# Keys evicted from PSUM once as f32 and split in SBUF, and one weighted sum per odd slot put in front of the transposed scores

## The reference

```python
x = _layernorm(x + attn(x, w_qkv, w_out, w_c1, w_c2))        # causal, rope, 56 tokens
x = _layernorm(x + xattn(x, ctx_2048, wq, bq, wkv, bkv, wp, bp))
x = _layernorm(x + ffn(x, gate_w, gate_b, w1, b1, w2, b2))   # top 2 of 8 experts

def xattn(x, cond, ...):                       # x (16, 56, 256), cond (16, 1500, 256)
    q = _qdq(x) @ _qdq(wq).T + bq              # int8 grid, as floats
    k, v = jnp.split(cond @ wkv.T + bkv, 2, axis=-1)
    # 16 heads of 16
    attn = jax.nn.softmax(jnp.einsum('bnhd,bmhd->bhnm', q, k) * scale, axis=-1)
    o = jnp.einsum('bhnm,bmhd->bnhd', attn, v)
    return _qdq(o) @ _qdq(wp).T + bp
```

## Time and profile before

| | |
|---|---|
| median of 3 runs | 853.0 us (848.32 to 858.43) |
| profiled execution, its own time | 854.35 us |
| its span, first to last instruction | 852.5 us |
| busy: PE, DVE, ACT, POOL | 774.4, 638.2, 511.5, 296.9 us |
| granted PE clock, mean | 0.986 |
| cross-attention, about | 50 to 690 us |

### The profile page before, as it was taken

The page is one execution under the profiler, slowest core; times in us unless marked ns, Lnnn a source line. Parts: engine busy times, 40 slices in busy tenths (PEclk is TensorE's granted clock), DMA queues, the critical chain, the costliest instruction groups (busy, mean ns, idle before and its releaser), DMA issues.

```text
span 852.5 us, 30042 instructions
## 1 busy us (share of the span) xinstructions
PE 774.4 (91%) x12379; PEld 582.8 (68%) x12379; DVE 638.2 (75%) x1234; ACT 511.5 (60%) x1084; POOL 296.9 (35%) x366
## 2 busy tenths in 40 slices
PE   5689989999998999999999999999898899999996
PEld 3366666576666666666666666666665579999995
DVE  5877777868877878785977778786875745688887
ACT  2347656566565657655665666666665543787772
POOL 3263216223712371254126421732270003143232
PEclk9899999999999999999999999999999899999999
DMA  7356554554645546554655655565467976766643
GB/s 228 91 167 174 169 155 139 156 160 128 179 129 159 164 143 180 164 143 138 178 156 141 173 169 147 154 171 156 121 186 208 307 258 161 225 190 209 210 136 98
DMA packets 91380, 143.27 MB, mean 168 GB/s; under 512 B 11423, under 2 KB 79583, under 8 KB 87918
## 3 DMA queue, kind: packets, MB, share of 16 engines
q1 hardware_dynamic: 87742, 136.74, 53.6%
q0 software_dynamic: 3504, 4.62, 2.8%
HBM read 101.60 MB, written 39.68 MB: 166 GB/s over the span
## 4 chain that ended last, share of the span: by engine, by line
PE 57%; DVE 13%; DMA 11%; ACT 10%; issue 6%; SPq 1%; POOL 1%; DVEq 0%; POOLq 0%; ACTq 0%
PE ps L1659 15%; PE ps L1652 11%; DMA sums<-y_sb,g_token 10%; PE ps L1733 7%; PE ps L1711 6%; DVE negmax L522 4%; ACT pT L1441 3%; ACT k_front L1414 3%; PE ps L1971 3%; PE ps L1675 3%; DVE k_front L516 2%; PE ps L1992 2%; PE ps L1776 2%; PE ps L1620 2%; PE ps L1743 2%
## 5 line engine op out<-in xcount | busy, mean ns | idle before, releaser
L522 DVE TENSOR_REDUCE negmax<-ps 112x1 f32<-112x1500 f32 x121 | 207.4, 1714 | 32.1 <-PE ps L1675 31.9
L1441 ACT ACTIVATE pT<-ps 125x448 f32<-125x448 f32 x384 | 195.7, 546 | 21.9 <-PE ps L1711 18.2
L1265 POOL TENSOR_TENSOR ctx_lo<-ctx_raw,ctx_hi 128x250 f16<-128x250 f32 x188 | 119.3, 666 | 182.4 <-DVE ctx_hi L507 182.4
L1711 PE MATMUL ps<-qbd,k_st 97*128 97x112 f16 x1536 | 127.8, 214 | 17.3 <-ACT pT L1441 8.7
L1711 PEld LDWEIGHTS ps<-qbd,k_st 97*128 97x128 f16 x1536 | 91.2, 98 | 73.6 <-ACT pT L1441 20.1
L1397 ACT COPY v_sb<-ps 125x512 f32<-125x512 f32 x96 | 56.4, 587 | 83.5 <-PE ps L1659 83.4
L516 DVE SCALAR_TENSOR_TENSOR k_front<-ps,bk_sb,k_front 128x500 f16<-128x500 f32 x80 | 58.8, 735 | 63.0 <-ACT k_front L1414 63.0
L1733 PE MATMUL ps<-pT,v_sb 125*17 125x56 f32 x6144 | 92.1, 215 | 12.2 <-issue 12.2
L1733 PEld LDWEIGHTS ps<-pT,v_sb 125*17 125x17 f32 x6144 | 79.9, 98 | 31.9 <-issue 20.1
L1414 ACT ACTIVATE k_front<-ps,bk_sb 128x500 f16<-128x500 f32 x80 | 54.3, 678 | 62.3 <-PE ps L1652 62.3
L1659 PE MATMUL ps<-wkv_hi,ctx_hi 128*125 128x256 f16 x384 | 76.6, 281 | 10.5 <-DVE k_front L516 9.0
(11 more groups left out here) (263 smaller groups left out, 1492.7 us busy)
## 6 DMA issues: line engine op xcount, KB each, us to landing
k_st<-k_dram SPq DMA_DIRECT2D x288, 125.0 KB, 3.0
w_sb<-w SPq DMA_DIRECT2D x25, 1024.0 KB, 5.2
ctx_raw<-ctx_T SPq DMA_DIRECT2D x48, 500.0 KB, 3.7
k_dram<-k_front SPq DMA_DIRECT2D x80, 250.0 KB, 3.0
xs<-zeros SPq DMA_DIRECT2D x28, 260.0 KB, 4.4
w_sb<-w SPq DMA_DIRECT2D x8, 512.0 KB, 5.2
k_dram<-k_back SPq DMA_DIRECT2D x16, 250.0 KB, 2.9
xg<-xs SPq DMA_DIRECT2D x21, 130.0 KB, 4.1
```

The lines of the kernel that those rows point to most:

```text
L522: V.tensor_reduce(negmax[0:QW], ps[0:QW, BANK_S:BANK_S + CHUNKS, 0:MC], AX.XY, ALU.max, negate=True).then_inc(max_done, 1)
L1265: last = nc.gpsimd.tensor_tensor(ctx_lo[:, k, c2, a], ctx_raw[:, k, c2, a], ctx_hi[:, k, c2, a], ALU.subtract)
L1441: nc.scalar.activation(pT[0:MT, (PAIRS * b + p) % 3, TPC * g:TPC * g + TPC], ps[0:MT, BANK_T + n % 2, 0:TPC * QW].rearrange("p (t n) -> p ...
L1711: last = mm(ps[:, BANK_T + n % 2, QW * i:QW * i + QW], k_st[:, j, p, a:a + P], qbd[:, j, p].rearrange("p h s -> p (h s)"), start=True, sto ...
```

## The change

1. ACT evicts a key unit once, as f32 with its bias, into `k_full` (three buffers), and this alone frees the PSUM bank.
2. DVE copies `k_full` to f16 for the high part; the low part is `k_full` minus the high part, both in SBUF. GpSimd makes it in two halves of 250 columns (`k_lo_step`), but DVE does for batch 0 (`key_low`), and for units 0 and 2 of every odd batch: both together in slot 3 of the even batch before, behind the maximum of pair 3.
3. The parts go into three buffers `k_two` instead of six. A store now waits for the low part (`k_lo_done`), the high part for the store of three keys before, ACT for the low part of three keys before.
4. In odd slots PE does the weighted sum of pair p - 2 in front of the transposed scores; only that of pair p - 1 stays behind the unit. Slot 3 of even batches keeps the old order.

```diff
@@ -159,14 +159,15 @@
         a_xqT = sb("a_xqT", [P, CH, P], BF16)
         wkv_hi = sb("wkv_hi", [P, CH, 2 * D], F16)
         wkv_lo = sb("wkv_lo", [P, CH, 2 * D], F16)
-        k_front = sb("k_front", [P, 5, 2, MC], F16)
+        k_two = sb("k_two", [P, 3, 2, MC], F16)
+        k_full01 = sb("k_full01", [P, 2, MC])
         sb("behind_k_front", [P, 8], F32)
         ctx_raw = sb("ctx_raw", [P, 2, CH, MC])
         ctx_hi = sb("ctx_hi", [P, 2, CH, MC], F16)
         ctx_lo = sb("ctx_lo", [P, 2, CH, MC], F16)
         q_st = sb("q_st", [KS, PAIRS, P], F16)
         k_st = sb("k_st", [KA, 2, PAIRS, M + 4], F16)
-        k_back = sb("k_back", [P, 2, MC], F16)
+        k_full2 = sb("k_full2", [P, MC])
         sb("behind_keys", [P, 616])
         q_mx = sb("q_mx", [KS, 2, PAIRS, 2, S], F16)
         v_sb = sb("v_sb", [P, 2, M // MT, H, VW])
...
@@ -219,7 +220,7 @@
         b_x2T = a_t2[:, 0:D].rearrange("p (c n) -> p c n", c=CH)
         b_oqT = a_t2[:, D:D + P].bitcast(BF16).rearrange("p (c n) -> p c n", c=CH)
-        k_two = [k_front[:, n] for n in range(5)] + [k_back]
+        k_full = [k_full01[:, 0], k_full01[:, 1], k_full2]
         staging = pT[:].rearrange("p a m n -> p (a m n)")
         wkv_raw = staging[:, 0:CH * 2 * D].rearrange("p (c n) -> p c n", c=CH)
...
@@ -433,10 +435,13 @@
             return CH * c + g
-        def stored(b, u):
-            n = KEY_UNITS.index(u)
-            return k_out[n % 2], 16 * (len(KEY_UNITS) // 2 * b + n // 2 + 1)
+        def key_number(b, u):
+            return len(KEY_UNITS) * b + KEY_UNITS.index(u)
+        def stored(n):
+            return k_out[n % 2], 16 * (n // 2 + 1)
         def loaded(b):
...
@@ -509,12 +514,21 @@
             def unit_step(b, par, u):
                 c, g = UNIT[u]
                 if g in KEYS:
-                    i = key_place(c, g)
-                    dve.wait_ge(unit_done, UNITS * b + u + 1)
-                    dve.wait_ge(k_hi_done, len(KEY_UNITS) * b + KEY_UNITS.index(u) + 1)
-                    V.scalar_tensor_tensor(k_two[i][:, 1], ps[:, BANK_KV, 0:MC], bk_sb[:, g:g + 1], k_two[i][:, 0],
-                                           ALU.add, ALU.subtract).then_inc(unit_out, 1)
+                    n = key_number(b, u)
+                    dve.wait_ge(unit_out, UNITS * b + u + 1)
+                    if n >= 3:
+                        dve.wait_ge(*stored(n - 3))
+                    V.tensor_copy(k_two[:, n % 3, 0], k_full[n % 3]).then_inc(k_hi_done, 1)
+                    if b == 0:
+                        key_low(b, u)
+            def key_low(b, u):
+                n = key_number(b, u)
+                dve.wait_ge(k_hi_done, n + 1)
+                dve.wait_ge(k_lo_done, n)
+                V.tensor_tensor(k_two[:, n % 3, 1], k_full[n % 3], k_two[:, n % 3, 0], ALU.subtract).then_inc(k_lo_done, 1)
             def max_step(b, p):
                 n = PAIRS * b + p + 1
...
@@ -859,6 +873,10 @@
                     if units_on:
                         for u in unit_slots(slot):
                             unit_step(b + 1, 1 - j, u)
+                    if slot == 3 and j == 0:
+                        key_low(b + 1, 0)
+                        key_low(b + 1, 2)
                     if t_before is not None:
                         b_tail(bt_behind, t_before)
                     if slot == 1 and units_on:
...
@@ -1080,11 +1098,11 @@
             def store_keys(b, u, between=()):
                 c, g = UNIT[u]
-                i = key_place(c, g)
-                sp.wait_ge(unit_out, UNITS * b + u + 1)
+                i, n = key_place(c, g), key_number(b, u)
+                sp.wait_ge(k_lo_done, n + 1)
                 if not (isinstance(b, int) and b == 0):
                     sp.wait_ge(k_in[g], loaded(b - 1))
-                sp.dma_start(k_dram[i], k_two[i]).then_inc(stored(b, u)[0], 16)
+                sp.dma_start(k_dram[i], k_two[:, n % 3]).then_inc(stored(n)[0], 16)
                 for dst, src in between:
                     sp.dma_start(dst, src).then_inc(w2_ahead, 16)
...
@@ -1325,23 +1347,46 @@
             pool.wait_ge(set_pe, 5)
             nc.gpsimd.memset(v_sb[:, 1, :, :, DH:VW], W_UP).then_inc(ones_v, 1)
+            def k_lo_step(b, u):
+                n = key_number(b, u)
+                pool.wait_ge(k_hi_done, n + 1)
+                if b % 2 == 1 and u == 5:
+                    pool.wait_ge(k_lo_done, n)
+                for half in range(2):
+                    a = slice(MC // 2 * half, MC // 2 * half + MC // 2)
+                    last = nc.gpsimd.tensor_tensor(k_two[:, n % 3, 1, a], k_full[n % 3][:, a], k_two[:, n % 3, 0, a], ALU.subtract)
+                last.then_inc(k_lo_done, 1)
             def iteration(it, t_before):
-                ctx_lo_step(2 * it + 1, 1, 1)
+                b = 2 * it + 1
+                ctx_lo_step(b, 1, 1)
                 if it > 1:
                     scatter(it - 2)
                 if it > 0:
                     pool.wait_ge(b_oq_done, it)
                 kbd_step(it + 1)
-                ctx_lo_step(2 * it + 1, 1, 2)
-                ctx_lo_step(2 * it + 2, 0, 0)
+                ctx_lo_step(b, 1, 2)
+                k_lo_step(b, 5)
+                k_lo_step(b, 6)
+                k_lo_step(b, 8)
+                ctx_lo_step(b + 1, 0, 0)
                 if t_before is not None:
                     b_rstd_step(t_before)
-                ctx_lo_step(2 * it + 2, 0, 1)
+                k_lo_step(b, 11)
+                ctx_lo_step(b + 1, 0, 1)
+                k_lo_step(b + 1, 0)
+                k_lo_step(b + 1, 2)
                 rstd_step(it + 1)
-                ctx_lo_step(2 * it + 2, 0, 2)
+                ctx_lo_step(b + 1, 0, 2)
+                k_lo_step(b + 1, 5)
+                k_lo_step(b + 1, 6)
+                k_lo_step(b + 1, 8)
                 qbd_step(it + 1, 0, 0)
-                ctx_lo_step(2 * it + 3, 1, 0)
+                ctx_lo_step(b + 2, 1, 0)
                 qbd_step(it + 1, 0, 1)
+                k_lo_step(b + 1, 11)
                 for h in range(2):
                     qbd_step(it + 1, 1, h)
...
@@ -1373,7 +1418,10 @@
             ctx_lo_step(B - 1, 1, 1)
             scatter(TILES - 3)
             ctx_lo_step(B - 1, 1, 2)
+            k_lo_step(B - 1, 5)
             b_rstd_step(TILES - 2)
+            for u in (6, 8, 11):
+                k_lo_step(B - 1, u)
             scatter(TILES - 2)
             pool.wait_ge(sums_set, 16 * TILES)
...
@@ -1406,13 +1454,12 @@
             def k_hi_step(b, u):
                 c, g = UNIT[u]
-                i = key_place(c, g)
-                if b > 0:
-                    act.wait_ge(*stored(b - 1, u))
+                n = key_number(b, u)
                 act.wait_ge(unit_done, UNITS * b + u + 1)
-                nc.scalar.activation(k_two[i][:, 0], ps[:, BANK_KV, 0:MC], ACT.Identity,
-                                     bias=bk_sb[:, g:g + 1]).then_inc(k_hi_done, 1)
+                if n >= 3:
+                    act.wait_ge(k_lo_done, n - 2)
+                nc.scalar.activation(k_full[n % 3], ps[:, BANK_KV, 0:MC], ACT.Identity, bias=bk_sb[:, g:g + 1]).then_inc(unit_out, 1)
             def v_step(b, par, u):
...
@@ -1897,6 +1944,11 @@
                         if t_before is not None:
                             b_over(2 if PAIRS * j + slot == 8 else B_SLOTS.get(PAIRS * j + slot - 1, -1), t_before)
                         a_step(A_AT.get(PAIRS * j + slot, -1), t_next)
+                    if not even and not (slot == 3 and j == 0):
+                        if p > 0:
+                            pv(b, j, p - 2)
+                        elif b > 0:
+                            pv(b - 1, 1 - j, PAIRS - 2)
                     scores_T(b, j, p, 0)
                     scores_T(b, j, p, 1)
                     if slot == 2 and j == 0 and b > 0:
...
@@ -1909,7 +1961,7 @@
                     else:
                         for u in us:
                             unit(b + 1, 1 - j, u)
-                        for q in (p - 2, p - 1):
+                        for q in (p - 2, p - 1) if slot == 3 and j == 0 else (p - 1,):
                             if q >= 0:
                                 pv(b, j, q)
                             elif b > 0:
```

9 lines of the change are left out of this document (7 added, 2 removed).

## The result

| | before | after |
|---|---|---|
| median, us | 853.3 (848.3 to 858.4, 4 runs) | 892.0 (888.7 to 893.1, 4 runs) |
| ratio | | 1.0447 (95% interval 1.0379 to 1.0515) |
| profiled execution, us | 854.35, span 852.5 | 888.71, span 886.9 |
| granted clock, mean | 0.986 | 0.959 |

The kernel became slower by 38.7 us. The forecast was 878, the range 852 to 897.

The account below looks back on a forecast made before the run. PE's own work plus a few short gaps per batch was taken to bound the kernel. Gains - 28, stops + 38, other waits + 2 and clock + 13 gave + 25 on 854.35: 879, or 878 on the median's scale; range 852 to 897.

Parts of the forecast that it names:

- The stop: Slot 4 of even batches: PE's scores wait for unit 11's load behind unit 0's store; 4.5 us, 7 times, 38 with batch 14.
- I take 1.36: 312.92: Batch 6, slot 3: DVE's low part beside GpSimd's work takes 1.36 us and ends at 312.92 on the trace's clock.
- the 3.7 without contention: Lower bound of the slot 4 stop, with 0.69 us for the low part and a 2.9 us landing.
- Batch 14, priced 6.5: The stop in batch 14, where pieces of weights are loaded among the keys: 6.5 us of PE standing.
- The other new waits: Slot 8 of even batches waits about 0.3 us each, 2 in all; odd batches' pair 4 nothing, at most 1 us each.
- The clock: One half-clock stretch of PE behind each of eight stops, 1.7 us each, 13 us; bounds 0 and twice that.
- Rival 1: The stops are there but the clock does not fall behind them: 865 us; chance 0.16.
- rival 2: No difference: stops at their lower bound, gains at 36, little from the clock: 853 us; chance 0.12.
- The gains: PE gaps removed at key evictions and transposed scores, in even and odd slots: 28 us, bounds 20 and 43.
- the cover behind the unit: Behind slots 1 and 5, cover shrinks from 1.9 us to 1.25; ACT needs 0.95, so cost nothing.
- rival 4: GpSimd late too: odd batches wait 1 us at pair 4, slot 8 costs 0.8, stops of 5.5; 897 us, chance 0.09.
- Rival 3: Faster: the load of unit 11 is covered after all, 827 us if fully covered; chance 0.08.

Follow-up runs that it names:

- experiment 1: The changed kernel with the load of unit 11 issued ahead of the store of unit 0; 833.9 us, ratio 0.9723 to the kernel before.
- experiment 5: The kernel before with SyncE made to hold the store of unit 0 of odd batches, nothing else; 919.3 us, ratio 1.0750.
- experiment 4: The changed kernel with GpSimd's kbd products waiting for the low parts of units 0 and 2; 878.6 us, ratio 1.0256 to the kernel before.
- experiment 3: The changed kernel with the weighted sums of odd slots put back where they were; 910.8 us, ratio 1.0618 to the kernel before.

## Why the prediction held, and where it did not

**The stop** was right in place, cause and count: experiment 1 removes it by the order of load and store alone, experiment 5 makes it with nothing else. Its size was not. The step that failed is "I take 1.36: 312.92" for the low part: L564, from which it was taken, was let in behind one GpSimd instruction of 0.93 us, while this one was held through a run of four, 3.7 to 4.1 us in batches 4 to 12. It took 2.4 us longer than forecast in batch 6, and the stops there are 6.2 to 7.5 us in place of 4.5. Where it was not held so long (batches 0 and 2: both low parts in 2.15 and 2.51 us) the stops are 3.6 and 4.5 us, and without the hold 3.2 to 4.4 (experiment 4): there my 4.5, and the 3.7 without contention, are what was seen. Batch 14, priced 6.5, measured 6.7. Eight stops: 38 forecast, 49.4 measured.

**The other new waits,** 2 us forecast and at most 1 us each in odd batches: six short ones, 4.3 us. Three are in odd batches at pair 4 (1.0, 0.94 and 0.42 us) and three in slot 8 of odd batches (0.69, 0.88 and 0.32); slot 8 of even batches, where the 2 us were put, has none.

**The clock,** 13 us forecast: it fell behind all eight stops, PE busy + 15.8 us. The rule of the Trainium skill (TensorE: Matmul & The Clock Gate, "What's actually happening") that full clock goes with recent activity agrees: eight of eight at 0.50 to 0.59. The count that I held against it, one in some ten, came from gaps of 1.5 us, a fifth of these. Rival 1 falls, and rival 2 with it, which needed stops at their lower bound and hardly any half clock.

**The gains,** 28 us: the waits and the clock are read from the profiled executions, so they go against the growth of the span, 886.9 - 852.5 = 34.4, and not against the 38.7 of the medians: 49.4 + 4.3 + 15.8 - 34.4 = 35.1 were there. By slots, per batch:

- Column 3 of even batches (the unit of slot 2): 0.70 of 0.74. Slots 1 and 2 of odd: 0.44 + 0.50 = 0.94 of 0.83. Both also in experiment 3, so they are the keys' own.
- Odd slot 5: 0.60 of 0.7. Even slot 7: 0.49 of 0.62. Odd slot 7: 0.45 of 0.37, and odd slot 6: 0.14 of some 0.3, both of them the keys' (they are in experiment 3 too). The 0.3 was not read rightly: of the 9.0 us 1.1 are left and not 1.5, which is 0.16 a batch.
- Given back, which I had at nothing: column 2, 6 and 7 of even batches + 0.23, + 0.12 and + 0.13, column 4 of odd + 0.23. All four are absent in experiment 3, so the cost is the sums': the cover behind the unit that I had called sufficient.

In all 0.7 us an even and 1.9 an odd batch, 18 us in 14 batches against 24.5 forecast. The remaining 17 lie outside these slots: 10.6 us are issue gaps in front of the sums (12.2 to 1.6), which I read in the earlier trace rows and took as fixed; the half clock behind one is in it too, and the rest is not divided further.

**The number.** Trace against trace the forecast was + 25 and the result + 34.4. It was short by 11.4 for the stops, 2.3 for the other waits and 2.8 for the clock, and the gains were 7.1 larger than forecast. So the total was nearer than its largest term by luck: gains that I had not seen paid for most of the hold that I had not seen. Odd batches became 1.9 us shorter, as forecast, but even ones 8.0 us longer and not 4 to 5.

**The rivals.** 892 lies between the forecast and rival 4 (897), and of that one the condition on slot 8 and the odd batches held only by half; what made the stops longer than 5.5 us was DVE's hold, no lateness of GpSimd. Rival 3, the load covered, is experiment 1 in effect: 834 to its 827; the 1.15 us that the hold costs in column 5, once no stop covers it, are about that difference over the even batches.

The rule on contention (the Trainium skill, SBUF — State Buffer, "Who interferes with whom": the later of the two blocks until the other is through) had the right direction. Read word for word it gives at most the rest of one product, about 1 us; the trace shows the rest of all four in five batches, and less in two.

## What to carry to other kernels

When a change gives a store, or any queued instruction, a new and later wait, look first at what stands behind it in the same queue: here a load of another batch, whose own data had long been ready, paid 3.6 to 7.5 us each time, and exchanging two issues was worth some 60 us. Price an operation that shares a resource against the whole run of the other engine's instructions, not against one. And after a stop is removed, expect the work that it covered to appear: here the late maximum, then the late products, then the context's low part.
